# Attention by pairs of head pairs, and eight places for rounded products in a feed-forward pass

## The chip, the cores and the metric

The kernel runs on one core of one Trainium2 chip. The metric is the time of one execution in microseconds of device time (us). Lower is better. The core has five engines that run side by side and wait for each other through semaphores: PE (TensorE, matrix products and transposes through PSUM), DVE (VectorE), ACT (ScalarE), POOL (GpSimd) and SP (which here issues DMAs).

## The reference

Sixteen sequences of 128 tokens and width 256 go through one gated cross-attention layer and one gated, quantised feed-forward layer.

```
q, k, v   = heads of layernorm(x) Wq, ctx Wkv          # 16 heads of 64
k, v      = with one null key and value put in front    # 129 keys
out       = softmax(q k^T / 8) v, then Wout
x         = x + tanh(g_xattn) * layernorm(out) * ln_scale + ln_bias (gated too)
h         = act_qdq(layernorm(x))                       # one scale over the whole tensor
up, gate  = act_qdq(h w_up^T), act_qdq(h w_gate^T)      # 4 bit weights, 16 bit activations
gate      = act_qdq(gate * fixed_qdq_u16(sigmoid(gate)))
o         = act_qdq(gate * up)                          # the scale needs the maximum over all of o
x         = x + tanh(g_ffn) * (o w_down^T)
```

## The kernel before

**Attention.** The sixteen sequences are eight groups of two (`g` from 0 to 7; groups 1 to 5 are one loop body, groups 0, 6 and 7 are written out). The sixteen heads are eight head pairs (`c` from 0 to 7, `NS = 8`): two heads of 64 fill the 128 partitions. For a head pair the work goes from engine to engine:

- PE `scores(g, c)`: eight products of 64 rows into two PSUM banks of the pair's parity (`c % 2`).
- DVE `maxima(g, c)`: two reductions. ACT `exps(g, c)`: four exponentials with their row sums into `probs[c % 2]`. DVE `inverse_sums(g, c)`. POOL `normalise(g, c)`.
- PE `prob_transposes(g, c)`: four transposes into the one bank `pt_bank`. DVE `prob_copy(g, c)`: copies that bank into `pT[c % 2]`, and with this frees it.
- PE `values(g, c)`: eight products onto 64 columns of the array, into `pv_bank`. ACT `out_high` and DVE `out_low` split the result into two addends of reduced precision in `oT` (this split makes up for the precision of a float32r product; every projection is three products).

**What fills PE between.** Between these short pieces PE works off units of projections for the next group, in a hand-written order, `PLAN`. `Q0` to `Q7` make queries and keys (18 products of 256 columns), `V00` to `V11` values (12 products of 512 columns), `X` transposes of the normalised input, `F0` to `F8` transposes of the feed-forward weights in the last group, `W` the output projection (50 products). In the loop body steps 0 to 4 hold one `Q` each, step 5 holds `Q5` and `V00`, step 6 `Q6` and `V10`, step 7 `Q7` and `X`, and `V01`, `V11` and `W` are the tail. Group 6 holds `Q0` to `Q4`, `V00`, `Q5`, `Q6`, and `V10` and `W` as its tail. `unit` writes the banks `unit_bank`.

**DVE's work beside it.** Per step DVE also does one piece of the layernorms: in step 1 `attention_rstd`, in step 2 `attention_norm`, in step 3 `x2_statistics`, in step 4 `ln_stats`, in step 5 `ln_rstd`, in step 6 `ln_apply`. Groups 0 and 6 round one feed-forward weight each in three steps instead (`weight_scales`, `weight_integers`, `weight_values`; lines 1156 to 1160, 1165 and 1170). After `W` comes `attention_stats`. In this text a piece of this kind is DVE's side work of step `c`.

Each engine runs its instructions strictly in the order of the program; only semaphores tie them together.

**Feed-forward.** After the attention, the feed-forward layer makes `gate` and `up` (all 2048 tokens in SBUF, 24 pieces of 128x512 each) and goes over them in three passes, since each quantisation needs a maximum over everything. The third pass is the last part of the kernel. For piece `n` of 24 it needs the rounded product as int16, `oint(n)`: for even pieces DVE makes it (`o_integers`, line 1497) from two other int16 tiles that ACT (line 971, and line 968 for every third) and DVE (line 1478) remake; for odd ones ACT makes it from `up` (`prepare`, line 963). Then ACT casts it to the high addend (line 785), DVE makes the low addend (line 995) and counts `ol_ready`, and PE multiplies both by `w_down`: 12 products of 256 columns a piece (`down`, line 760). For the last six pieces PE does three piece by piece and then waits for all that are left. `oint(n)` has four places, in `tui`: place `n` is written again once the low addend of piece `n - 4` is done, which the code says as a wait for `n - 3` on `ol_ready`.

Of the kernel before, what the change touches and what calls it, by code (L numbers as in the profile page):

```python
# [72 lines left out]
def gated_cross_attention_ffn(nc, x, ctx, g_xattn, g_ffn, Wq, Wkv, null_kv, Wout, ln_scale, ln_bias,  # L73
                              w_gate, w_up, w_down, out):
    B, S, D = x.shape
# [32 lines left out]
    LOOPED = NG - 2  # L108

# [61 lines left out]
    with keep:  # L171
# [71 lines left out]
        GS = 6  # L243

# [232 lines left out]
        def oint(n):  # L477
            return tui[:, 2 + n % 4 // 2, n % 2 * HC:(n % 2 + 1) * HC]
# [75 lines left out]
        def _(pe):  # L554
# [8 lines left out]
            def unit(g, pos):  # L563
# [74 lines left out]
                else:  # L638
                    pe.wait_ge(w_free, g + 1)
                    for b in range(GB):  # L640
# [3 lines left out]
                        if b == 0:  # L644
                            wait(pe, ot_lo, g * NS + NS)
# [27 lines left out]
            def values(g, c):  # L673
                wait(pe, pt_copied, g * NS + c + 1)
                wait(pe, ot_lo, g * NS + c)
                for b in range(GB):
                    for h in range(2):
                        rows = slice(h * DH, (h + 1) * DH)
                        last = mm(pv_bank[rows, b * S:(b + 1) * S], v[:, b, c, rows],  # L679
                                  pT[:, c % 2, 2 * h + b, :], start=True, stop=True)  # L680
                last.then_inc(pv_done, 1)

            for pos in range(len(PRO)):
                unit("pro", pos)
                if PRO[pos] == "k6":
                    pe.wait_ge(null_ready, 1)
                    scores(0, 0)

            def group(g):
                final = isinstance(g, int) and g == NG - 1  # L690
                pos, (steps, tail) = 0, plan(g)
                for c in range(NS):
                    if c + 1 < NS:
                        scores(g, c + 1)
                    for _ in steps[c]:
                        unit(g, pos)
                        pos += 1
                    prob_transposes(g, c)
                    if c:
                        values(g, c - 1)  # L700
                if not final:
                    scores(g + 1, 0)
                values(g, NS - 1)
# [77 lines left out]
        def _(act):  # L781
# [27 lines left out]
            def out_high(g, c):  # L809
                wait(act, pv_done, g * NS + c + 1)  # L810
                high(oT[0][:, c, :], pv_bank[:, 0:TG]).then_inc(ot_hi, 1)
# [18 lines left out]
            while npos[0] < len(PRO):  # L830
                split("pro", npos[0])
                if PRO[npos[0]] == "k6":
                    exps(0, 0)
                if PRO[npos[0]] == "V11":
# [3 lines left out]
            def group(g):  # L838
                final = isinstance(g, int) and g == NG - 1
                pos, (steps, tail) = 0, plan(g)  # L840
                for c in range(NS):

                    weights = steps[c][0][0:1] == "F"
                    if c + 1 < NS and not weights:
                        exps(g, c + 1)
                    for _ in steps[c]:
                        split(g, pos)
                        pos += 1
                    if c + 1 < NS and weights:
                        exps(g, c + 1)  # L850
                    if c:
                        out_high(g, c - 1)
                if not final:
                    exps(g + 1, 0)
                out_high(g, NS - 1)
# [133 lines left out]
        def _(dve):  # L989
# [81 lines left out]
            def attention_stats(g, dst):  # L1071
# [9 lines left out]
                maxima(g + 1, 1)  # L1081
# [65 lines left out]
            def out_low(g, c):  # L1147
                dve.wait_ge(ot_hi, g * NS + c + 1)
                low(oT[1][:, c, :], pv_bank[:, 0:TG], oT[0][:, c, :]).then_inc(ot_lo, 1)
# [52 lines left out]
            while npos[0] < len(PRO):  # L1202
                if PRO[npos[0]] == "V00":
                    ln_stats(1)
                elif PRO[npos[0]] == "V10":
                    ln_rstd()
                elif PRO[npos[0]] == "V01":
# [6 lines left out]
                if PRO[npos[0]] == "k6":  # L1214
                    maxima(0, 0)
                    inverse_sums(0, 0)
# [4 lines left out]
            maxima(0, 1)  # L1221
            dve.wait_ge(const_ready, 1)

            def group(g):
# [3 lines left out]
                for c in range(NS):  # L1228
                    if 1 <= c < NS - 1:
                        maxima(g, c + 1)  # L1230
# [19 lines left out]
                    weights = steps[c][0][0:1] == "F"  # L1250
# [390 lines left out]
```

## Time and profile before

| | |
|---|---|
| time, median of 3 runs | 598.54 us (598.26 to 599.53) |
| the profiled execution's own time | 599.63 us |
| its span, first to last instruction | 597.6 us |
| PE busy | 524.0 us, 88% |
| DVE busy | 410.5 us, 69% |
| ACT busy | 298.4 us, 50% |
| POOL busy | 123.6 us, 21% |

The profiled execution took 2.0 us more than its span, and 1.1 us more than the median of the runs. The groups of the attention end at 99.7, 149.8, 199.9, 250.0, 300.1, 350.2, 392.2 and 431.4 us of the span, so one group of the loop body takes 50.1 us. The third feed-forward pass runs from 551 us to the end. Busy times of a PE whose products overlap are modelled, and so only a first hint. An engine's idle time costs something only where another engine waits for what comes late.

### The profile page before, as it was taken

How to read it: one execution, taken by the hardware profiler on the slowest of the kernel's cores; microseconds unless marked ns; L12 is line 12 of the kernel's file. 1: busy time of each engine (PE TensorE's matmuls, PEld its weight loads, DVE VectorE, ACT ScalarE, POOL GpSimd, SP SyncE). 2: the span in 40 equal slices, each digit the busy share in tenths (PEclk: the TensorE clock that was granted, in tenths of full speed). 3: DMA queues.
4: the chain of work that ended last, by engine and by line, in shares of the span. 5: the costliest groups of instructions: out<-in, count | busy, mean ns of one | idle time of the engine just before them, and what ended most of it. 6: DMA issues, size and time to landing. Idle time of an engine off the chain costs nothing. (4 is left out here: it accounts for less than half of the span.)

```text
span 597.6 us, 10965 instructions
## 1 busy us (share of the span) xinstructions
PE 524.0 (88%) x3921; PEld 456.4 (76%) x3921; DVE 410.5 (69%) x1077; ACT 298.4 (50%) x858; POOL 123.6 (21%) x137
## 2 busy tenths in 40 slices
PE   2999999999999999999999999997639999500997
PEld 2988889888988988888898898885528888400996
DVE  4779744754764574575476458658748989999685
ACT  3635532632542362363254335327325569897773
POOL 3001301220221130122022112213031029900000
PEclk9999999999999999999999999999959999855799
DMA  7922001101100110110110001005001000100033
GB/s 257 361 88 72 1 1 54 37 1 54 35 0 0 53 35 0 53 35 0 35 45 8 1 2 36 2 1 160 0 19 35 2 0 1 35 1 1 1 106 105
DMA packets 18478, 25.86 MB, mean 43 GB/s; under 512 B 1216, under 2 KB 15808, under 8 KB 18448
## 3 DMA queue, kind: packets, MB, share of 16 engines
q1 hardware_dynamic: 18192, 25.17, 12.8%
q0 software_dynamic: 256, 0.30, 0.2%
q8 instruction: 18, 0.29, 0.2%
q14 instruction: 12, 0.10, 0.1%
HBM read 21.27 MB, written 4.19 MB: 43 GB/s over the span
## 5 line engine op out<-in xcount | busy, mean ns | idle before, releaser
L804 ACT ACTIVATE probs<-bank,nmax 128x129 f32<-128x129 f32 x256 | 90.9, 368 | 117.8 <-DVE nmax L1132 117.7
L1551 POOL TENSOR_TENSOR probs<-probs,rinv 128x512 f32<-128x512 f32 x64 | 66.7, 1042 | 337.8 <-DVE rinv L1140 337.8
L607 PE MATMUL bank<-wv,ctxT 128*128 128x512 f32 x384 | 94.2, 397 | 0.0
L599 PE MATMUL bank<-ctxT,wk 128*128 128x256 f32 x672 | 88.9, 282 | 0.0
L599 PEld LDWEIGHTS bank<-ctxT,wk 128*128 128x128 f32 x672 | 83.6, 188 | 0.0
L607 PEld LDWEIGHTS bank<-wv,ctxT 128*128 128x128 f32 x384 | 70.5, 188 | 16.9 <-issue 1.2
L1144 DVE COPY pT<-bank 128x512 f32<-128x512 f32 x64 | 43.7, 682 | 20.7 <-PE bank L670 18.7
L599 PE MATMUL bank<-xnT,wq 128*128 128x256 f32 x336 | 54.7, 298 | 0.0
L785 ACT ACTIVATE oT<-bank 128x256 fp32r<-128x256 f32 x64 | 24.7, 386 | 60.0 <-PE bank L679 60.0
L804 ACT ACTIVATION_READ_ACCUMULATOR probs<-bank,nmax 128x1 f32 x256 | 52.0, 203 | 0.0
L599 PEld LDWEIGHTS bank<-xnT,wq 128*128 128x128 f32 x336 | 43.2, 188 | 7.2 <-issue 1.2
L1132 DVE TENSOR_REDUCE nmax<-bank 128x2 f32<-128x258 f32 x128 | 48.0, 416 | 0.0
L785 ACT ACTIVATE qk<-bank 128x512 f32<-128x512 f32 x64 | 38.4, 599 | 18.7 <-PE bank L599 13.6
L648 PE MATMUL bank<-wout,oT 128*128 128x256 f32 x384 | 47.1, 279 | 0.0
L1059 DVE TENSOR_TENSOR v<-bank,nvb 128x512 f32<-128x512 f32 x32 | 22.1, 690 | 35.7 <-PE bank L607 35.6
L648 PEld LDWEIGHTS bank<-wout,oT 128*128 128x128 f32 x384 | 46.0, 188 | 0.3
L662 PE MATMUL bank<-qk 64*128 64x130 f32 x512 | 45.9, 297 | 0.0
L679 PE MATMUL bank<-pT,v 128*64 128x128 f32 x512 | 42.1, 285 | 3.7 <-DVE oT L995 3.7
L760 PE MATMUL bank<-wd,oI 128*128 128x256 f32 x288 | 39.2, 298 | 5.4 <-DVE oI L995 5.2
L760 PEld LDWEIGHTS bank<-wd,oI 128*128 128x128 f32 x288 | 37.5, 204 | 7.2 <-DVE oI L995 6.5
L670 PE MATMUL bank<-ident,probs 128*128 128x128 f32 x256 | 38.6, 273 | 4.2 <-POOL probs L1551 4.2
L662 PEld LDWEIGHTS bank<-qk 64*128 64x128 f32 x512 | 33.6, 186 | 10.6 <-issue 9.2
(170 smaller groups left out, 810.6 us busy)
## 6 DMA issues: line engine op xcount, KB each, us to landing
craw<-in_ctx SPq DMA_DIRECT2D x8, 512.0 KB, 3.3
stage<-in_L_xattn_Wkv SPq DMA_DIRECT2D x8, 512.0 KB, 11.9
xa<-in_x SPq DMA_DIRECT2D x8, 256.0 KB, 2.7
xr<-in_x SPq DMA_DIRECT2D x8, 256.0 KB, 2.8
x_scratch<-y SPq DMA_DIRECT2D x7, 256.0 KB, 2.1
x2all<-x_scratch SPq DMA_DIRECT2D x1, 1792.0 KB, 8.3
xres<-x_scratch SPq DMA_DIRECT2D x6, 256.0 KB, 2.8
out<-yout SPq DMA_DIRECT2D x6, 256.0 KB, 2.2
```

The lines of the kernel that those rows point to most:

```text
L599: last = mm(bk[:, n * TG:(n + 1) * TG], wt[a][:, k, f], act_t[b][:, k, :], start=(k == 0 and i == 0), stop=(k == kk - 1 and i == len(TERMS ...
L607: last = mm(bk[:, :], ctxT[a][:, k, b * S:(b + 1) * S], wv[w][:, k, h * 512:(h + 1) * 512], start=(k == 0 and i == 0), stop=(k == KC - 1 a ...
L648: last = mm(o, oT[a][:, k, b * S:(b + 1) * S], wout[w][:, k, :], start=False, stop=(k == KF - 1 and i == len(TERMS) - 1))
L662: last = mm(score_bank[c % 2][h][:, b * QW:b * QW + QW], qk[rows, c, b, 0:S], qk[rows, c, GB + b, 0:QW], start=True, stop=True)
L670: last = nc.tensor.transpose(pt_bank[:, u * P:(u + 1) * P], probs[:, c % 2, u, 0:S], ident[:, :])
L679: last = mm(pv_bank[rows, b * S:(b + 1) * S], v[:, b, c, rows], pT[:, c % 2, 2 * h + b, :], start=True, stop=True)
L760: last = mm(bank[tg % 2 * 4 + t][:, 0:D], oI[a][:, tg % 2, j, t * P:(t + 1) * P], wd[w][:, j, :], start=(j == 0 and i == 0), stop=(j == KI ...
L785: return nc.scalar.activation(dst, src, act_copy, scale=scale)
L804: last = nc.scalar.activation(probs[:, c % 2, u, 0:NK], score_bank[c % 2][h][:, b * QW:b * QW + NK], ACT.Exp, bias=nmax[:, c % 2, u:u + 1] ...
L1132: last = V.tensor_reduce(nmax[:, c % 2, 2 * h:2 * h + 2], score_bank[c % 2][h][:, 0:GB * QW].rearrange("p (b s) -> p b s", b=GB)[:, :, 0:N ...
L1144: V.tensor_copy(pT[:, c % 2, :, :], pt_bank[:, :].rearrange("p (u s) -> p u s", u=4)).then_inc(pt_copied, 1)
L1551: G.tensor_tensor(probs[:, c % 2, :, 0:S], probs[:, c % 2, :, 0:S], rinv[:, c % 2, :].rearrange("p (u o) -> p u o", o=1).to_broadcast([P, ...
```

## The change

**In attention** the loop over eight head pairs becomes one over four pairs of them, `p` from 0 to 3 (`PAIRS = 4`). PE issues the scores of two head pairs in a row, and the two `values` in a row; `pv_bank` now takes both results (512 columns), and `out_high`, `out_low` are one instruction for both. Between stand the transposes of head pair `2p`, its units, the transposes of `2p + 1` and its units. The softmax of a head pair starts one pair ahead. On DVE the two `maxima` stand at the start of the pair, the side work (`beside(c)`) is put ahead of `prob_copy(g, c)`, and `inverse_sums` comes behind it. The last group issues its scores singly.

**In the third pass** `oint(n)` gets eight places, in `tpi` (which the second pass has done with), and the two waits for `n - 3` become waits for `n - 7`.

```diff
+    PAIRS = NS // 2
+        OR = 8
...
         def oint(n):
-            return tui[:, 2 + n % 4 // 2, n % 2 * HC:(n % 2 + 1) * HC]
+            return tpi[:, n % OR // 2, n % 2 * HC:(n % 2 + 1) * HC]
...
-            def values(g, c):
-                wait(pe, pt_copied, g * NS + c + 1)
-                wait(pe, ot_lo, g * NS + c)
...
+            def values(g, p):
+                wait(pe, pt_copied, g * NS + 2 * p + 2)
+                wait(pe, ot_lo, g * PAIRS + p)
...
@@ PE, group(g)
-                for c in range(NS):
-                    if c + 1 < NS:
-                        scores(g, c + 1)
-                    for _ in steps[c]:
-                        unit(g, pos)
-                        pos += 1
-                    prob_transposes(g, c)
-                    if c:
-                        values(g, c - 1)
-                if not final:
-                    scores(g + 1, 0)
-                values(g, NS - 1)
+                for p in range(PAIRS):
+                    to = (g, 2 * p + 2) if p + 1 < PAIRS else (None if final else (g + 1, 0))
+                    if to:
+                        scores(to[0], to[1])
+                        if not final:
+                            scores(to[0], to[1] + 1)
+                    for n in range(2):
+                        if n and to and final:
+                            scores(to[0], to[1] + 1)
+                        prob_transposes(g, 2 * p + n)
+                        for _ in steps[2 * p + n]:
+                            unit(g, pos)
+                            pos += 1
+                    values(g, p)
...
@@ DVE, group(g)
+                for p in range(PAIRS):
+                    to = (g, 2 * p + 2) if p + 1 < PAIRS else (None if final else (g + 1, 0))
+                    if to and not final:
+                        maxima(to[0], to[1])
+                        maxima(to[0], to[1] + 1)
+                    for n in range(2):
+                        c = 2 * p + n
+                        if to and final:
+                            maxima(to[0], to[1] + n)
+                        beside(c)
                         prob_copy(g, c)
-                        out_low(g, c - 1)
...
+                        if to:
+                            inverse_sums(to[0], to[1] + n)
+                        for _ in steps[c]:
+                            split(g, pos)
+                            pos += 1
+                    out_low(g, p)
...
@@ third pass, ACT and DVE
-                    wait(act, ol_ready, n - 3)
+                    wait(act, ol_ready, n - OR + 1)
...
-                wait(dve, ol_ready, n - 3)
+                wait(dve, ol_ready, n - OR + 1)
```

How PE's order moves in the loop body, at steps 3 and 4. L662 is `scores`, L599 the unit `Q`, L670 the transposes, L679 `values`. Before:

```order
L670 MATMUL bank<-ident,probs 128x128 [waits pt_copied,norm_done]
L679 MATMUL bank<-pT,v 64x128 [waits ot_lo,pt_copied]
L662 MATMUL bank<-qk 128x130 [waits exp_done]
L599 MATMUL bank<-xnT,wq 128x256 [waits unit_hi]
L599 MATMUL bank<-ctxT,wk 128x256 x12
...
L670 MATMUL bank<-ident,probs 128x128 [waits pt_copied,norm_done]
```

The same stretch now (L664, L601, L672 and L683 are the same four), over one whole pair:

```order
L664 MATMUL bank<-qk 128x130 [waits exp_done]
...
L664 MATMUL bank<-qk 128x130 [waits exp_done]
...
L672 MATMUL bank<-ident,probs 128x128 [waits pt_copied,norm_done]
...
L601 MATMUL bank<-xnT,wq 128x256 [waits unit_hi]
...
L672 MATMUL bank<-ident,probs 128x128 [waits pt_copied,norm_done]
...
L601 MATMUL bank<-xnT,wq 128x256 [waits unit_hi]
...
L683 MATMUL bank<-pT,v 64x128 [waits ot_lo,pt_copied]
```

Between one set of transposes and the next there stood the values, the scores and a unit; between the first and the second set of a pair there now stands a unit alone.

How DVE's order moves in the loop body at step 2 (oT is `out_low`, nmax `maxima`, rs and y the side work `attention_norm`, rinv `inverse_sums`, pT `prob_copy`). Before:

```order
L995 TENSOR_TENSOR oT<-bank,oT 128x256
L1132 TENSOR_REDUCE nmax<-bank 128x2 x2
L1006 SCALAR_TENSOR_TENSOR rs<-rs 128x2
...
L1105 SCALAR_TENSOR_TENSOR y<-y,rs,xr 128x256 x2
L1140 RECIPROCAL rinv<-rowsum 128x4
L1144 COPY pT<-bank 128x512
L995 TENSOR_TENSOR oT<-bank,oT 128x256
```

And now, from `out_low` of pair 0 to the copy of head pair 2:

```order
L998 TENSOR_TENSOR oT<-bank,oT 128x512
...
L1134 TENSOR_REDUCE nmax<-bank 128x2 x2
...
L1134 TENSOR_REDUCE nmax<-bank 128x2 x2
L1009 SCALAR_TENSOR_TENSOR rs<-rs 128x2
...
L1107 SCALAR_TENSOR_TENSOR y<-y,rs,xr 128x256 x2
L1146 COPY pT<-bank 128x512
L1142 RECIPROCAL rinv<-rowsum 128x4
```

Ahead of the copy there now stand the wide `out_low` of the pair before, twice the maxima and the side work.

## Rows read from the trace of the kernel before

**Rows 1.** The page: busy tenths of PE in 40 slices of the span.

```profile
PE   2999999999999999999999999997639999500997
```

**Rows 2.** Waits of PE over the span: us in total, times, longest.

```profile
PE bank L670 <- POOL probs L1551: 4.2, 4, 1.4
PE bank L679 <- DVE oT L995: 3.7, 8, 1.0
```

**Rows 3.** Timeline of PE in a body step: start, length, what.

```profile
206.10 0.60 PE L670 MATMUL bank<-ident,probs 128*128 128x128 f32 x4
206.63 0.66 PE L679 MATMUL bank<-pT,v 128*64 128x128 f32 x8
207.22 0.72 PE L662 MATMUL bank<-qk 64*128 64x130 f32 x8
...
208.69 1.58 PE L599 MATMUL bank<-ctxT,wk 128*128 128x256 f32 x12
210.11 0.60 PE L670 MATMUL bank<-ident,probs 128*128 128x128 f32 x4
```

**Rows 4.** Timeline of PE cut inside the scores that end at 207.94.

```profile
207.55 0.39 PE L662 MATMUL bank<-qk 64*128 64x130 f32 x4
...
207.66 0.28 PE L662 MATMUL bank<-qk 64*128 64x130 f32 x2
```

**Rows 5.** Timeline of DVE and PE at a wait of PE for DVE.

```profile
187.01 0.42 DVE L995 TENSOR_TENSOR oT<-bank,oT 128x256 fp32r<-128x256 f32 x1 [0.32 <-ACT oT L785]
187.35 0.68 DVE L995 TENSOR_TENSOR xnT<-bank,xnT 128x512 fp32r<-128x512 f32 x1
...
187.59 0.66 PE L679 MATMUL bank<-pT,v 128*64 128x128 f32 x8 [0.39 <-DVE oT L995]
```

**Rows 6.** Timeline of DVE in a body group.

```profile
199.89 0.76 DVE L1079 BATCH_NORM_STATS2 bn<-bank 128x6 f32<-128x256 f32 x2 [3.52 <-PE bank L648]
...
201.62 0.88 DVE L1089 SCALAR_TENSOR_TENSOR y<-bank,mv,gs 128x256 f32<-128x256 f32 x2
...
208.10 0.75 DVE L1132 TENSOR_REDUCE nmax<-bank 128x2 f32<-128x258 f32 x2
208.76 0.15 DVE L1006 SCALAR_TENSOR_TENSOR rs<-rs 128x2 f32<-128x2 f32 x1
...
210.92 0.17 DVE L1140 RECIPROCAL rinv<-rowsum 128x4 f32<-128x4 f32 x1
...
216.77 0.74 DVE L1028 BATCH_NORM_STATS2 bn<-xa 128x6 f32<-128x256 f32 x2
...
217.64 0.15 DVE L1032 BATCH_NORM_AGGREGATE mv<-bn 128x2 f32<-128x6 f32 x1
```

**Rows 7.** Timeline of DVE: weights in groups 0 and 6.

```profile
51.26 1.76 DVE L1170 TENSOR_TENSOR fraw<-fint,fs 128x1536 f32<-128x1536 int16 x1
...
367.06 1.74 DVE L1156 TENSOR_REDUCE fs<-fraw 128x48 f32<-128x1536 f32 x1
...
369.55 0.18 DVE L1140 RECIPROCAL rinv<-rowsum 128x4 f32<-128x4 f32 x1
```

**Rows 8.** The page's groups: copies out of PSUM.

```profile
L1144 DVE COPY pT<-bank 128x512 f32<-128x512 f32 x64 | 43.7, 682 | 20.7 <-PE bank L670 18.7
...
L785 ACT ACTIVATE qk<-bank 128x512 f32<-128x512 f32 x64 | 38.4, 599 | 18.7 <-PE bank L599 13.6
```

**Rows 9.** Timeline of PE in the third pass.

```profile
553.87 23.48 PE L760 MATMUL bank<-wd,oI 128*128 128x256 f32 x168 [3.64 <-DVE oI L995]
...
562.25 11.71 PE L760 MATMUL bank<-wd,oI 128*128 128x256 f32 x96
...
590.28 4.57 PE L760 MATMUL bank<-wd,oI 128*128 128x256 f32 x36 [0.89 <-DVE oI L995]
```

**Rows 10.** Busy by stretch: length, PE, PEld, DVE, ACT, POOL; PEclk, DMA share, GB/s.

```profile
560.00:573.96 13.96, 13.96 (x117) 13.75 (x115) 11.45 (x20) 10.92 (x19) 0.00 (x0) 1.00 0.15 47
573.96:590.28 16.32, 14.56 (x108) 13.30 (x108) 13.00 (x24) 11.48 (x20) 0.00 (x0) 1.00 0.32 96
```

More of the change, by code:

```diff
@@ L644, in unit @@
                         if b == 0:
[L645 removed]
+                            wait(pe, ot_lo, g * PAIRS + PAIRS)
                         for k in range(KF):
@@ L671, in prob_transposes @@
                 last.then_inc(pt_done, 1)
-            def values(g, c):
-                wait(pe, pt_copied, g * NS + c + 1)
-                wait(pe, ot_lo, g * NS + c)
[L676 to L680, printed above, removed]
+            def values(g, p):
[3 more added lines that the diff above has]
+                    c = 2 * p + n
+                    for b in range(GB):
+                        for h in range(2):
+                            rows = slice(h * DH, (h + 1) * DH)
+                            last = mm(pv_bank[rows, n * TG + b * S:n * TG + (b + 1) * S], v[:, b, c, rows],
+                                      pT[:, n, 2 * h + b, :], start=True, stop=True)
                 last.then_inc(pv_done, 1)
@@ L687, in _ @@
                     scores(0, 0)
+                    scores(0, 1)
             def group(g):
@@ L840, in group @@
                 pos, (steps, tail) = 0, plan(g)
[L841 to L855, printed above, removed]
+                for p in range(PAIRS):
+                    to = (g, 2 * p + 2) if p + 1 < PAIRS else (None if final else (g + 1, 0))
+                    for n in range(2):
+                        if to:
+                            exps(to[0], to[1] + n)
+                        for _ in steps[2 * p + n]:
+                            split(g, pos)
+                            pos += 1
+                    out_high(g, p)
                 for u in tail:
@@ L1215, in _ @@
                     maxima(0, 0)
-                    inverse_sums(0, 0)
+                    maxima(0, 1)
                 if PRO[npos[0]] == "V11":
@@ L1227, in group, with beside @@
                 pos, (steps, tail) = 0, plan(g)
-                for c in range(NS):
-                    if 1 <= c < NS - 1:
-                        maxima(g, c + 1)
+                def beside(c):
                     if c == 1 and not first:
@@ L1555, in _ @@
             normalise(0, 0)
+            normalise(0, 1)
             pool.wait_ge(const_ready, 1)
             def group(g):
-                for c in range(1, NS):
+                for c in range(2, NS):
                     if c == 6:
```

44 lines of the change are left out of this document (19 added, 25 removed).

## The prediction

> **What bounds the kernel now.** I read the slices first [rows 1]. PE's row is nines from the third slice to the 28th, so up to about 420 us PE decides, and after that it does in parts only. The waits say the same [rows 2]: over the whole span PE waited 3.7 us for `out_low` ahead of `values` (eight times, one a group) and 4.2 us for POOL ahead of transposes, the latter in four places of the last group. A group of the loop body takes 50.1 us and PE stands still for some 0.4 us of it. So in attention the change can only gain by making PE's own work shorter, and it loses whatever new wait it puts on PE. DVE has time to spare over a group, but what counts is when a single copy comes. In the third pass the timeline shows PE fed until 573.96 and then with holes, until it gets the last 36 products at 590.28 [rows 9].
>
> **What PE saves.** Ends of blocks are the measure, since one block's start overlaps the last one's end. From one end to the next [rows 3]: values 207.29 - 206.70 = 0.59 us, scores 207.94 - 207.29 = 0.65, unit Q 210.27 - 207.94 = 2.33, transposes 210.71 - 210.27 = 0.44; 4.01 for a step. Inside the scores, four products on two row halves take 0.39 and two take 0.28, so two cost 0.11 and all eight would take 0.44 [rows 4]. The same 0.11 for two products of 128 columns makes values 0.44. So the first products after a change of the array's shape cost extra: 0.15 for values (128x64), 0.21 for scores (64x128); the unit has no inside row here, and I take 0.20, so 2.13 without it. That is 0.56 a step for three changes, 0.19 each.
>
> Counting blocks in the two orders, a body group enters a new shape 25 times before (scores 8, values 8, full array 9) and 13 times after. Groups 0 to 6 save 12 each, the last saves 5 (23 to 18). 12 x 0.19 = 2.3 us a group. With the wait of 0.4 for `out_low` at the end of a group, which goes since the two results now leave together [rows 2], that is 2.7 us for each of seven groups.
>
> The Trainium skill says this too: TensorEngine Tiling (Array Packing), section Tiling Modes, states that changing the tiling mode drains the engine. The trace agrees, with the 0.15 to 0.21 above. Taken alone the rule says that half the changes is a faster kernel, and that is the rival below.
>
> **What PE loses.** Between the first and the second transposes of a pair there is now only one unit Q. The second ones write `pt_bank`, so they wait for DVE's copy of the first. DVE comes to this copy late: it must first do `out_low` of the pair before, which cannot start before `values` is over, then four reductions, then the side work of the even step.
>
> From the end of `values` to the end of the second transposes, on DVE's path: to ACT 0.04, `out_high` with 512 columns 0.60 (as the copy of a unit [rows 8]), to DVE 0.04, `out_low` 0.60 until the next can start (a low part of 512 columns is 0.68 long [rows 5]; a following instruction starts 0.08 before its end), two `maxima` 2 x 0.66 = 1.33 (208.10 to 208.76 [rows 6]), the side work B, the copy 0.68 [rows 8], then DVE to PE 0.15 and the block 0.66 (`oT` ends at 187.43, `values` starts at 187.59 [rows 5]). The sum is 4.10 + B. The handover to PE includes the weight load, which starts some 0.04 earlier, so I take 4.07 + B.
>
> On PE's own path: scores 0.65 + 0.44, transposes 0.44 + 0.15 for the change, unit 2.13, transposes 0.44: 4.25. So the wait is B - 0.18 when only one unit Q is in between.
>
> B in a body group [rows 6]: step 2, `attention_norm`, 208.76 to 210.92, 2.16, a wait of 2.0. Step 4, `ln_stats`, 216.77 to 217.79, 1.0, a wait of 0.8. Step 6 has V10 behind Q6, 2.8 us more of cover, no wait. Step 0 has no side work, but DVE comes from `attention_stats` of the group before: from the end of `W` 0.04, then 199.89 to 202.50 less the `maxima` inside and the overlap, 1.9, then 1.33, 0.68, 0.11 and 0.66, 4.7 against 4.25: 0.4. Together 3.2 us a group, against 2.7 saved. A body group becomes 0.5 us longer: five of them, +2.5.
>
> Side work of odd steps stands ahead of the second copy, which `values` waits for behind one more unit. `ln_rstd`, the longest, has Q5 and V00 in front of it; no wait. The softmax of a head pair now starts a pair (7 to 8 us) ahead; its exponentials wait for the transposes that free `probs`, its sum of ACT, DVE and POOL pieces is under 4 us, so it is not late in the body.
>
> Group 6: steps 4 to 6 round a weight. Step 4 is 2.5 us (367.06 to 369.55 [rows 7]), a wait of 2.3; step 6 is 1.7 (a 1.75 long instruction), with one Q in between here, 1.5; step 2 2.0; step 0 0.4. 6.2 - 2.7 = +3.5. Group 0: step 0 has 1.7 of weight work (51.26 [rows 7]), and DVE enters the group some 0.9 late, 1.1; step 1 has the 2.5 one, which makes the first `values` wait 0.5; step 2 1.5; step 4 0.8. 3.9 - 2.7 = +1.2.
>
> The last group is paced by the softmax chain. It has five changes less (1.0) and its first scores were issued before it (0.65), but the chain of a pair makes both the copy and `values` wait. Its waits now are 5 us [rows 2], and I estimate 0.7 more. -1.0, with bounds of -3 (no more waits) and +2.
>
> Attention: 1.2 + 2.5 + 3.5 - 1.0 = **+6.2 us**. The prologue gets the scores of head pair 1, 0.45 us, inside a stretch in which PE waits for DVE's weight work; nothing.
>
> **The third pass.** At full speed a product takes (11.71 - 0.28) / 95 = 0.12 us, a piece 1.44 [rows 9]. From 573.96 to the last end, 594.85, there are 12 pieces: 20.9 us against 17.3, so 3.6 us of holes. The rest of the pass PE was fed. Do DVE and ACT keep up, if the ring no longer stops them? From 560 to 590.28 they made the low parts of pieces 4 to 23: DVE was busy 24.45 us, 1.22 a piece, ACT 22.4, 1.12 [rows 10]. Both are below 1.44. Eight places give four more pieces of lead, so PE becomes the bound and its holes close: **-3.6 us**. Bounds: 0 if something else paces them, and -4.5 if the first pieces, which take PE longer (168 products in 23.48), run faster too. What comes after PE's last product is unchanged.
>
> **Sum:** 6.2 - 3.6 = +2.6 us. The profiled execution was 599.63, so one like it would take 602.2; against the median of the runs, 598.54 + 2.6 = **601.1 us**. A measurement of this kernel can tell about 0.2%, 1.2 us, from no change.
>
> **Rivals.**
> - *Faster: the changes of shape decide.* If DVE's copy came before PE needs it, attention would gain 2.7 x 7 + 1 to 2, some 20 us, and with the pass the kernel would take 575. For it: the saving is in PE's own rows. Against it: it needs B to be below 0.2 at steps 2 and 4, and B is 2.2 and 1.0 in the trace. In between, the sign turns where the waits are 2.6 us less over the program, that is 0.4 a group: an `out_high` or a handover that is a little quicker than I took, or a change that costs 0.22 instead of 0.19. Then 595 to 597.3. 0.12.
> - *No change to be told.* The same two sums, but each off by 1 to 2 us: 597.4 to 599.7. 0.20.
> - *Slower by more: the pass gives nothing.* If DVE's order (`finish` waits for PE's tiles) paces the third pass, or if the waits also reach `values` in the body, 604 to 606. Against it: DVE's busy share. 0.08.
> - *Slower as summed,* 599.8 to 604: 0.60.
>
> So slower has 0.68. The range of 597.4 to 604 leaves out the faster end and the part of the worst above 604. The unknown costs inside it: the change into `values` after a unit and into transposes after scores (0 to 0.21 each, some 30 of each, taken as 0.15), and the width of `out_high`.
>
> **What would show it.** In the profile after: a body group of 50.6 us in place of 50.1; PE waiting for DVE's copy (`pT`) ahead of transposes, three times a group, longest near 2.0, some 20 us in all plus 6 in group 6, with DVE's `values` wait gone from the body; two scores blocks back to back in 1.1 us from end to end, two `values` in 1.0; group 6 near 45.5 us. In the third pass PE's row without holes behind 574 and ACT's wait for DVE's `oI` gone; PE's last product 3.6 us earlier relative to its first. I am wrong if PE's waits for the copy stay under 2 us a group, or if the holes of the third pass stay.

## The result and the profile after

| | before | after |
|---|---|---|
| median of the runs | 599.03 us (598.26 to 599.65, 4 runs) | 605.75 us (602.39 to 609.66, 4 runs) |
| the profiled execution: time, span, mean granted clock | 599.63, 597.6, 0.951 | 605.15, 603.1, 0.951 |

The ratio is 1.0102, with an interval of 1.0068 to 1.0137. So the kernel became slower, as forecast, but by 6.7 us at the median and not by 2.6, and the median lies above the range that was given (597.4 to 604.0).

The page of the profile after. Its first line is the span, then the busy time of each engine, then two of the rows in 40 slices:

```profile
span 603.1 us, 10904 instructions
PE 509.5 (84%) x3921; PEld 453.5 (75%) x3921; DVE 412.7 (68%) x1045; ACT 295.5 (49%) x826; POOL 126.5 (21%) x137
...
PE   2998899899899989989998998798738999800698
PEclk9999999999999999999999999899877999965699
```

The row of nines of [rows 1] now has eights all through attention. PE waits there in every group. The 26th digit of the clock's row (377 to 392 us) and the 29th (422 to 437) are eights, in the last two groups of attention; this comes back below.

The waits of PE over the span (us in total, times, longest), kernel after:

```profile
PE bank L672 <- DVE pT L1146: 23.7, 25, 2.1
...
PE bank L683 <- DVE pT L1146: 6.2, 8, 2.3
PE bank L767 <- DVE oI L998: 3.6, 1, 3.6
```

The two rows of [rows 2] are gone: no wait for `out_low` and none for POOL. In their place PE waits for DVE's copy `pT`, 23.7 us ahead of transposes (L672), and 6.2 us ahead of values (L683). Of the third pass only the wait at its start is left.

PE in one body group (151.4 to 202.6), timeline: start, length, what, and the idle time ahead of it:

```profile
151.32 1.17 PE L664 MATMUL bank<-qk 64*128 64x130 f32 x16
152.42 0.66 PE L672 MATMUL bank<-ident,probs 128*128 128x128 f32 x4
...
155.58 0.63 PE L672 MATMUL bank<-ident,probs 128*128 128x128 f32 x4 [0.36 <-DVE pT L1146]
...
158.68 1.09 PE L683 MATMUL bank<-pT,v 128*64 128x128 f32 x16 [0.34 <-DVE pT L1146]
159.70 1.17 PE L664 MATMUL bank<-qk 64*128 64x130 f32 x16
...
165.34 0.63 PE L672 MATMUL bank<-ident,probs 128*128 128x128 f32 x4 [1.75 <-DVE pT L1146]
...
173.68 0.63 PE L672 MATMUL bank<-ident,probs 128*128 128x128 f32 x4 [0.70 <-DVE pT L1146]
```

Two scores now stand together (x16, and the next block begins 1.10 us behind their start), and two values too (158.68 to 159.70 by the starts, 1.02). The waits stand at steps 0, 2 and 4, where they were expected, and at one more place: the values of pair 0, at 158.68. This group takes 51.2 us, the five of the loop 51.1 on average.

PE in the third pass, timeline, kernel after:

```profile
563.45 36.93 PE L767 MATMUL bank<-wd,oI 128*128 128x256 f32 x288 [3.64 <-DVE oI L998]
```

All 288 products are one row without a hole. From the first start to the last end it is 36.93 us; in [rows 9] it was 594.85 - 553.87 = 40.98.

**Where the 5.5 us between the two profiled executions are.** I put the ends of the eight groups (the last end of the output products, L650) of both traces side by side. After: 100.3, 151.4, 202.6, 253.7, 304.9, 356.0, 403.0, 441.8. Before: 99.7, 149.8, 199.9, 250.0, 300.1, 350.2, 392.2, 431.4.

| stretch | before | after | difference | predicted |
|---|---|---|---|---|
| prologue and group 0 | 99.7 | 100.3 | +0.7 | +1.2 |
| five body groups, each | 50.1 | 51.1 | +1.03, together +5.1 | +0.5, together +2.5 |
| group 6 | 42.0 | 47.0 | +5.0 | +3.5 |
| last group | 39.2 | 38.7 | -0.5 | -1.0 |
| from there to the first product of the third pass | 122.5 | 121.7 | -0.8 | 0 |
| third pass, first start to last end | 40.98 | 36.93 | -4.05 | -3.6 |
| sum | | | +5.5 | +2.6 |

(The signs are right wherever one was forecast. The rows are rounded, the sum is not.) Two rows are off by over a microsecond: the body groups by 2.6, group 6 by 1.5.

### The profile page after: what moved, and what is told of

Read it like the earlier page. It is cut to its first block and busy times, and to the rows that moved or that the text cites. A ratio compares the mean times of both kernels' runs of the same rounds, so it can differ in the third digit from the quotient of the medians.

```text
span 603.1 us, 10904 instructions
## 1 busy us (share of the span) xinstructions
PE 509.5 (84%) x3921; PEld 453.5 (75%) x3921; DVE 412.7 (68%) x1045; ACT 295.5 (49%) x826; POOL 126.5 (21%) x137
## 5 line engine op out<-in xcount | busy, mean ns | idle before, releaser
L1551 POOL TENSOR_TENSOR probs<-probs,rinv 128x512 f32<-128x512 f32 x64 | 69.6, 1088 | 344.0 <-DVE rinv L1142 343.9
L609 PE MATMUL bank<-wv,ctxT 128*128 128x512 f32 x384 | 95.6, 402 | 0.0
L601 PE MATMUL bank<-ctxT,wk 128*128 128x256 f32 x672 | 89.0, 282 | 0.0
L601 PEld LDWEIGHTS bank<-ctxT,wk 128*128 128x128 f32 x672 | 83.8, 188 | 0.0
L672 PE MATMUL bank<-ident,probs 128*128 128x128 f32 x256 | 41.7, 286 | 23.7 <-DVE pT L1146 23.7
L1062 DVE TENSOR_TENSOR v<-bank,nvb 128x512 f32<-128x512 f32 x32 | 22.0, 689 | 48.9 <-PE bank L609 48.9
L601 PE MATMUL bank<-xnT,wq 128*128 128x256 f32 x336 | 53.9, 296 | 0.0
L672 PEld LDWEIGHTS bank<-ident,probs 128*128 128x128 f32 x256 | 27.8, 143 | 33.2 <-issue 28.5
L998 DVE TENSOR_TENSOR oT<-bank,oT 128x512 fp32r<-128x512 f32 x32 | 22.1, 691 | 39.3 <-ACT oT L792 39.3
L650 PE MATMUL bank<-wout,oT 128*128 128x256 f32 x384 | 47.3, 279 | 0.0
L650 PEld LDWEIGHTS bank<-wout,oT 128*128 128x128 f32 x384 | 46.2, 188 | 0.3
L1134 DVE TENSOR_REDUCE nmax<-bank 128x2 f32<-128x258 f32 x128 | 45.6, 416 | 0.0
L601 PEld LDWEIGHTS bank<-xnT,wq 128*128 128x128 f32 x336 | 43.6, 189 | 0.0
L683 PE MATMUL bank<-pT,v 128*64 128x128 f32 x512 | 35.0, 279 | 6.3 <-DVE pT L1146 6.2
L767 PE MATMUL bank<-wd,oI 128*128 128x256 f32 x288 | 36.9, 294 | 3.6 <-DVE oI L998 3.6
L664 PE MATMUL bank<-qk 64*128 64x130 f32 x512 | 38.1, 285 | 0.0
```

The lines of the kernel that those rows point to most:

```text
L601: last = mm(bk[:, n * TG:(n + 1) * TG], wt[a][:, k, f], act_t[b][:, k, :], start=(k == 0 and i == 0), stop=(k == kk - 1 and i == len(TERMS ...
L609: last = mm(bk[:, :], ctxT[a][:, k, b * S:(b + 1) * S], wv[w][:, k, h * 512:(h + 1) * 512], start=(k == 0 and i == 0), stop=(k == KC - 1 a ...
L650: last = mm(o, oT[a][:, k, b * S:(b + 1) * S], wout[w][:, k, :], start=False, stop=(k == KF - 1 and i == len(TERMS) - 1))
L664: last = mm(score_bank[c % 2][h][:, b * QW:b * QW + QW], qk[rows, c, b, 0:S], qk[rows, c, GB + b, 0:QW], start=True, stop=True)
L672: last = nc.tensor.transpose(pt_bank[:, u * P:(u + 1) * P], probs[:, c % 2, u, 0:S], ident[:, :])
L683: last = mm(pv_bank[rows, n * TG + b * S:n * TG + (b + 1) * S], v[:, b, c, rows], pT[:, n, 2 * h + b, :], start=True, stop=True)
```

## The experiments

Each ratio is against runs of the kernel before on the same chip. The first four below shared one chip and one set of such runs (599.32 us, 11 runs), the next four a second chip (598.28 us, 11 runs), and the last two a third (599.71 us, 9 runs).

### The same kernel again

No edit; more runs, to see the scatter and a second profile.

> The changed kernel once more, to see how its time scatters. Its first four runs took 602.4 to 609.7 us, where the kernel before took 598.3 to 599.7. Theory A (PE's new waits let the granted clock fall, at places that differ from run to run): again a scatter of 4 us or more, a longer time going with a lower mean clock, and in the profile short stretches at half clock between 355 and 442 us. Theory B (the waits alone make the time): the scatter stays under 2 us and the time does not follow the clock.

Measured: 605.14 us (602.55 to 606.41, 6 runs), ratio 1.0089 [1.0067, 1.0110]. In the second profile the body groups were 51.07 to 51.17 and group 6 was 47.06. I had tied the time of a run to its mean granted clock. That holds only loosely: 606.41 us came at 0.946 and 602.55 at 0.951, but 604.00 at 0.954. The groups repeat to 0.1 us, and the median is 5.8 to 6.7 us above before. The runs of this kernel scatter over 4 to 7 us, those of before over 1.4 to 3.2.

### Attention alone

The product ring goes back to four places, the rest of the change stays:

```diff
-        OR = 8
+        OR = 4
...
-            return tpi[:, n % OR // 2, n % 2 * HC:(n % 2 + 1) * HC]
+            return tui[:, 2 + n % 4 // 2, n % 2 * HC:(n % 2 + 1) * HC]
```

> The attention part alone; the rounded products of the third pass have four places again. If the two parts add up, it is slower than the changed kernel by what the third pass gained, 3.6 to 4.1 us: some 9 to 10 us above the kernel before, 608 to 610 us, with PE's holes behind the fifteenth piece of the third pass back. Rival: the gain of the third pass came from a clock that rose sooner because attention ended at another time; then it is within 1 us of the changed kernel.

Measured: 609.14 us (607.57 to 610.75, 5 runs), ratio 1.0173 [1.0152, 1.0195]. Attention alone costs 9.8 us at the median, not 6.2. Its third pass took 41.0 us from first start to last end and has the holes of [rows 9]. Its profiled execution (607.57 us) was the fastest of the five; there the prologue with group 0 is 1.2 us longer than before, the five body groups together 5.0, group 6 3.5, and the last group 0.9 shorter. The prediction had +1.2, +2.5, +3.5 and -1.0: in this profile the body groups alone are off.

### The third pass alone

Attention as before, the products of the third pass in eight places:

```diff
-            return tui[:, 2 + n % 4 // 2, n % 2 * HC:(n % 2 + 1) * HC]
+            return tpi[:, n % 8 // 2, n % 2 * HC:(n % 2 + 1) * HC]
```

with the waits for a free place moved from four products back to eight.

> The third pass alone: eight places, attention as in the kernel before. By the sum of the prediction 598.5 - 3.6 = 594.9 us, up to 594.4; PE's row in the third pass without holes. Rival (the eight places help only where the attention is by pairs): 598 to 599.

Measured: 595.59 us (593.21 to 596.30, 6 runs), ratio 0.9928 [0.9910, 0.9947], that is -3.7 us. The timeline of its third pass:

```profile
554.12 37.40 PE L760 MATMUL bank<-wd,oI 128*128 128x256 f32 x288 [3.64 <-DVE oI L995]
```

40.98 - 37.40 = 3.58 us. That term stood as summed, and so did its reason: before, ACT waited ten times for DVE's low part ahead of making a rounded product (L963), 7.6 us in all, and with eight places that wait is gone (in the profile after too). And the halves add up: +9.8 - 3.7 = +6.1, against +5.8 for the whole on the same chip. So the whole surprise is in attention.

### The copy ahead of the side work

The theory that DVE's side work (B) makes PE wait says that the copy, put first, brings back nearly all of it. A rival would be that two head pairs at a time cost PE something else, such as a softmax that comes too late; then the order on DVE would matter little.

```diff
-                        beside(c)
                         prob_copy(g, c)
+                        beside(c)
```

> The changed kernel with DVE's copy of the transposed probabilities ahead of its side work, in every step. Theory 1 (DVE's side work ahead of the copy is what makes PE wait, and the changes of the array's shape are a real saving): the waits of 1.7 and 0.7 us in a body group go, some 0.4 us at the group's start and at most 0.4 us ahead of the first values remain; a body group takes 51.1 - 3.9 + 0.5 to 0.9 = 47.7 to 48.1 us, group 6 40.5 to 41.5, and the kernel 575 to 580 us. Rival 2 (the wide copies out of PSUM and the four maxima alone make the copy late): groups stay above 50 us and the kernel above 598. Rival 3 (the shape changes save nothing, PE's row is only cut differently): about 595, that is the third pass alone.

Measured: 578.96 us (577.04 to 581.73, 6 runs), ratio 0.9659 [0.9633, 0.9685]: 26 us less than after, from one line. A body group takes 47.8 to 48.0, and group 6 takes 40.1, just below the expected 40.5 to 41.5. All waits of PE between 143 and 334 us, in this kernel:

```profile
PE bank L672 <- DVE pT L1146: 1.4, 4, 0.4
```

One wait of 0.4 is left per group, at step 0. The rival falls.

### The copy first in even steps only

```diff
+                        if n == 0:
+                            prob_copy(g, c)
                         beside(c)
-                        prob_copy(g, c)
+                        if n == 1:
+                            prob_copy(g, c)
```

This keeps the order of the odd steps, whose side work I had called free.

> The copy ahead of DVE's side work in even steps only; in odd steps the side work stays ahead. Theory 1 (the wait is the whole of the side work minus some 0.2 us, wherever it stands ahead of a copy that PE needs): the waits ahead of the second transposes go as with the copy first everywhere, but the side work of step 3 (1.3 us, behind that of step 2) now holds up the second copy and so the values of pair 1, by some 1.4 us; a body group 49.1 to 49.5 us, against 47.9 with the copy first everywhere and 51.1 in the changed kernel; the kernel 587 to 591. Rival (only the first copy matters, the second has a unit as cover): a body group as with the copy first everywhere, 48 us, the kernel 579.

Measured, on another chip (before 598.28): 592.72 us (591.22 to 594.71, 4 runs), ratio 0.9908 [0.9884, 0.9931]. The body group is 49.5 as expected; the kernel missed the expected 587 to 591 by 1.7 us, because group 6 only came down to 42.0 and the last group stayed at 39.0 (its clock fell there, beside a wait of 2.28). The waits of PE in a body group of this kernel (148.9 to 198):

```profile
PE bank L683 <- DVE pT L1146: 1.5, 2, 1.1
PE bank L672 <- DVE pT L1146: 0.4, 1, 0.4
```

Both waits of L683 are those of the values, which odd copies make. So the odd steps' side work wasn't free: with the even copies early, it costs 49.5 - 47.9 = 1.6 us a group, partly since PE now arrives at the values sooner.

### The first reciprocals of a pair later

Why do the values of pair 0 wait? DVE's timeline of the kernel after, at steps 0 and 1:

```profile
155.82 0.18 DVE L1142 RECIPROCAL rinv<-rowsum 128x4 f32<-128x4 f32 x1 [0.39 <-ACT probs L811]
155.91 0.14 DVE L1004 TENSOR_SCALAR rs<-mv 128x2 f32<-128x2 f32 x1
156.09 1.06 DVE L1005 TENSOR_SCALAR rs<-rs 128x2 int32<-128x2 int32 x1
157.18 0.16 DVE L1009 SCALAR_TENSOR_TENSOR rs<-rs 128x2 f32<-128x2 f32 x1
...
157.85 0.69 DVE L1146 COPY pT<-bank 128x512 f32<-128x512 f32 x1
```

and POOL's timeline there:

```profile
156.08 1.04 POOL L1551 TENSOR_TENSOR probs<-probs,rinv 128x512 f32<-128x512 f32 x1 [16.97 <-DVE rinv L1142]
```

The instruction of L1005 works on 128x2 elements and took 1.06 us. It begins 0.01 us behind POOL's multiply and ends 0.02 us behind POOL's end (157.12). The multiply waits for `inverse_sums` (L1142). That of the even step now stands right ahead of the side work of the odd step, so the two meet each time. If POOL holds this instruction back, then with these reciprocals behind the side work it should be short, and the wait of the values should go:

```diff
+                        if n == 1 and to:
+                            inverse_sums(to[0], to[1])
                         prob_copy(g, c)
-                        if to:
-                            inverse_sums(to[0], to[1] + n)
+                        if n == 1 and to:
+                            inverse_sums(to[0], to[1] + 1)
```

> The changed kernel with one instruction moved: the inverse sums of the first head pair of a pair stand behind the side work of the odd step instead of ahead of it, so POOL's multiplication starts when that side work is over. In the changed kernel the second small instruction of steps 1 and 5 took 1.06 us in every body group, and 0.17 in the kernel before; it began just before POOL's multiplication and ended just before it did. Theory A (POOL's multiplication holds up this DVE instruction): it is back to 0.17 us, the wait of 0.34 us ahead of the values of pair 0 goes, a body group 50.6 to 50.8 us in place of 51.1, the kernel 602 to 603.5. Rival B (the small instruction is slow for another reason, such as the place behind a wide copy): it stays at 1.06 us and the group at 51.1.

(By the rows above the instruction begins just behind the start of the multiply and ends just behind its end, not before them.)

DVE's timeline at the same place of this kernel:

```profile
155.22 0.16 DVE L1004 TENSOR_SCALAR rs<-mv 128x2 f32<-128x2 f32 x1
155.41 0.17 DVE L1005 TENSOR_SCALAR rs<-rs 128x2 int32<-128x2 int32 x1
...
156.21 0.18 DVE L1142 RECIPROCAL rinv<-rowsum 128x4 f32<-128x4 f32 x1
156.30 0.69 DVE L1146 COPY pT<-bank 128x512 f32<-128x512 f32 x1
```

And all waits of PE in its four groups from 151 to 354 us:

```profile
PE bank L672 <- DVE pT L1146: 11.2, 12, 1.8
```

L1005 is back to 0.17 us, there is no wait of values any more, and a body group takes 50.7 instead of 51.1. In the time of the kernel it can't be told: 602.98 us (601.10 to 605.17, 6 runs), ratio 1.0078 [1.0056, 1.0100], whose interval overlaps that of after. Five groups at 0.4 would be 2 us; the ratios differ by 0.0011, which is 0.7 us.

### The waits filled in the last two groups

The second thing that I had left out is the clock. This kernel adds products that nothing reads ahead of the late transposes of group 6 and the late values of the last group, so that PE has work in its waits:

```diff
+            def fill(g, p, count):
+                wait(pe, ot_lo, g * PAIRS + p)
+                for _ in range(count):
+                    mm(pv_bank[:, 0:256], wq[0][:, 0, 0:P], wq[0][:, 0, 0:256], start=True, stop=True)
...
+                        if isinstance(g, int) and g == NG - 2 and n == 1 and p:
+                            fill(g, p, (0, 12, 15, 9)[p])
...
+                    if final and p in (1, 2):
+                        fill(g, p, 15)
```

> The changed kernel with PE kept busy in its longest waits of the last two groups: 12, 15 and 9 products that nothing reads ahead of the second transposes of pairs 1 to 3 of group 6, and 15 each ahead of the values of pairs 1 and 2 of group 7. Each fill is shorter than the wait it stands in by its row. Theory A (these waits let the granted clock fall): no stretch at half clock between 350 us and the end of attention, group 6 45.4 to 45.6 us in the profile, group 7 under 38.3, the median 602 to 603.5 with a scatter under 2.5 us. Rival B (the clock falls for another reason, or costs nothing): scatter and median as in the changed kernel, 605.

Busy time by stretch of group 6, kernel after (length, then PE, PEld, DVE, ACT, POOL with their instructions, granted clock, share of DMA, GB/s):

```profile
376.00:380.00 4.00, 1.87 (x16) 1.65 (x15) 3.90 (x7) 1.51 (x8) 0.73 (x1) 1.00 0.00 0
380.00:384.00 4.00, 4.00 (x12) 2.87 (x10) 1.62 (x3) 1.49 (x8) 2.78 (x2) 0.57 0.00 0
384.00:388.00 4.00, 4.00 (x48) 3.56 (x48) 2.77 (x7) 1.28 (x5) 0.00 (x0) 1.00 0.00 0
```

The same stretch in the filled kernel:

```profile
380.00:384.00 4.00, 4.00 (x28) 3.19 (x30) 2.90 (x4) 1.51 (x8) 3.51 (x2) 1.00 0.00 0
```

And PE's timeline there, kernel after:

```profile
379.26 0.63 PE L672 MATMUL bank<-ident,probs 128*128 128x128 f32 x4 [2.13 <-DVE pT L1146]
379.64 4.59 PE L609 MATMUL bank<-wv,ctxT 128*128 128x512 f32 x12
```

then in the filled kernel:

```profile
377.71 1.95 PE L678 MATMUL bank<-wq 128*128 128x256 f32 x15
379.99 0.63 PE L672 MATMUL bank<-ident,probs 128*128 128x128 f32 x4 [0.33 <-DVE pT L1155]
380.38 3.04 PE L609 MATMUL bank<-wv,ctxT 128*128 128x512 f32 x12
```

Behind the wait of 2.13 us the granted clock is 0.57 as the mean of four microseconds, so for most of them the lower of its two levels (1.2 GHz) held, and the same twelve products took 4.59 us instead of 3.04. With the wait filled the clock stays at 1.00, and group 6 takes 45.5 us instead of 47.0. Attention alone (above) had no such fall in group 6 of its profile, behind a wait of 2.12 us, and its group 6 also took 45.5. The second profile of the changed kernel and that of the kernel with the later reciprocals had it there (group 6 47.1 and 46.9, waits of 2.13 and 2.12). So nearly the same wait brings the fall in some executions and not in others.

Measured: 603.59 us (602.78 to 604.83, 6 runs), ratio 1.0084 [1.0070, 1.0098]. The runs scatter over 2.0 us in place of 3.9 (the same kernel again) or 7.3 (the first four), but the median, 0.1 above the expected 602 to 603.5, isn't separated from that of after by these intervals.

### Both, the copy first and filled

The copy ahead of side work, and `fill` with 7 and 16 products ahead of the values of pairs 1 and 2 of the last group, again read by nothing.

> The copy first in every step, and 7 and 16 such products ahead of the values of pairs 1 and 2 in the last group, where that kernel waits 1.1 and 2.3 us and where its clock fell. If the falls are the reason for its scatter of 577.0 to 581.7: 576.5 to 577.5 us with a scatter under 2 us. Rival: no difference, 579.

Measured: 577.63 us (576.18 to 578.68, 5 runs), ratio 0.9649 [0.9632, 0.9667]. The last group takes 37.2 instead of 38.1, and no stretch of attention is at the lower clock. The median is just above the expected 576.5 to 577.5, the scatter 2.5 instead of under 2. The ratio isn't separated from that of the copy first alone (0.9633 to 0.9685), so what filling gives is read from the last group and not from the time of the kernel.

### The second scores moved back

To measure what a change of the array's shape costs, apart from waits, I took the kernel with the copy first and let the second scores of a pair stand behind the first transposes, in groups 0 to 6. That is two more changes a pair, eight a group.

```diff
                         scores(to[0], to[1])
-                        if not final:
-                            scores(to[0], to[1] + 1)
...
                         prob_transposes(g, 2 * p + n)
+                        if n == 0 and to and not final:
+                            scores(to[0], to[1] + 1)
```

> The kernel with the copy first in every step (578.96 us, a body group 47.9), with the second scores of a pair moved behind the first transposes of the pair, in groups 0 to 6. The same products; the array's shape changes twice more a pair. DVE still gets the second scores about when it is through with the first maxima. If a change of shape costs 0.15 to 0.21 us: 4 x 0.4 = 1.6 us more a group at least in PE's own work, a body group 49.3 to 49.9, the kernel 590 to 593. Rival (the saving came from fewer waits and handovers, not from the shape): the group stays within 0.4 us of 47.9 and the kernel within 3 us of 579.

Measured (before 599.71 here): 587.04 us (585.70 to 588.58, 4 runs), ratio 0.9802 [0.9771, 0.9832]. PE's timeline in a body group:

```profile
147.31 0.72 PE L664 MATMUL bank<-qk 64*128 64x130 f32 x8
147.95 0.66 PE L672 MATMUL bank<-ident,probs 128*128 128x128 f32 x4
148.54 0.72 PE L664 MATMUL bank<-qk 64*128 64x130 f32 x8
149.19 0.98 PE L601 MATMUL bank<-xnT,wq 128*128 128x256 f32 x6
```

A body group takes 49.0 us and PE waits nowhere in it. I had expected 49.3 to 49.9, since I didn't see that the wait of 0.4 at step 0 would go too: the scores in between give DVE that time. The kernel came below the expected 590 to 593.

The last group is the same here as with the copy first alone, and this profile has no fall of the clock in it, behind the same wait:

```profile
407.56 1.10 PE L683 MATMUL bank<-pT,v 128*64 128x128 f32 x16 [2.26 <-DVE pT L1146]
```

It took 37.2 us, as with the wait filled, and 38.1 with the copy first alone, where the clock fell. So that fall cost 0.9 us, and filling gained only what it cost.

### The copy ahead of the maxima

The last wait is that of step 0, so there the copy goes ahead of the maxima as well; the rest is as in the kernel with copy first and filled.

```diff
+                    early = p == 0 and not final
+                    if early:
+                        prob_copy(g, 0)
                     if to and not final:
                         maxima(to[0], to[1])
                         maxima(to[0], to[1] + 1)
...
-                        prob_copy(g, c)
+                        if c or not early:
+                            prob_copy(g, c)
                         beside(c)
```

> The kernel with the copy first and the last group's waits filled (577.63 us), with DVE's copy at the start of a group also ahead of the four maxima. It waits there 0.36 us in each of seven groups, for a copy that stands behind the statistics of the output and the maxima, 1.3 us. If that is the whole wait, it goes: 577.6 - 7 x 0.4 = 574.8 us. Rival (the later maxima make the exponentials and the first values late by as much): 577 to 578.

Measured, on the same chip: 574.43 us (573.63 to 575.12, 5 runs), ratio 0.9584 [0.9561, 0.9607]. This is the fastest kernel of the study, 4.2% faster than before. Its body group takes 47.42 us without a wait of PE. Neither kernel has a wait of PE in the body, so eight changes of shape cost 49.04 - 47.42 = 1.62 us, 0.20 each.

## Why the prediction was right and wrong

**What PE saves: right.** The term was 12 x 0.19 = 2.3 us a group. The body group of before without its wait is 50.1 - 0.4 = 49.7, that of the last experiment 47.4: 2.3 us. The price of one change, read from ends of blocks in [rows 3] and [rows 4], was 0.19; eight of them taken back cost 0.20 each. (If the wait of before also cost the 0.14 found below, 2.15 us are left for twelve changes, 0.18 each.)

**Where PE waits for the copy, and how long: right for even steps.** The idle times in the rows above are 0.36, 0.34, 1.75 and 0.70, together 3.15 us. The group lost 51.13 - 47.42 = 3.71, so each of the four waits costs about 0.14 more than the row shows as idle. The likely reason is the overlap of two blocks, which is lost as well: transposes that waited end 0.63 us behind their own start, and without a wait they end 0.44 behind the end of the block ahead of them. With it: 0.5 at step 0 (predicted 0.4, though its terms, 4.7 against 4.25, make nearly 0.5), 1.9 at step 2 (2.0), 0.8 at step 4 (0.8). That it is DVE's order and no late softmax is shown by the kernel with the copy first.

**The step that failed in the body.** "`ln_rstd`, the longest, has Q5 and V00 in front of it; no wait." The sum thus put the waits of `values` in the body at nothing. I looked at the longest side work of an odd step and not at `attention_rstd` in step 1, which has only one unit ahead of the values. It would have been in time by its own length; but POOL's multiply held one of its instructions back by 0.9 us, and the values of pair 0 waited 0.34 us by the row (0.48 with the overlap) in every group. This and the 0.1 us at step 0 make a group 1.03 us longer instead of 0.5, five groups 2.6 us. The reciprocals moved later took 0.4 us of this away, and the group of 50.7 that they leave is 3.3 us above the last experiment's, where the prediction had 3.2 of waits. The rows that could have warned me are in the trace of before:

```profile
170.67 0.29 DVE L1001 TENSOR_SCALAR rs<-mv 128x2 f32<-128x2 f32 x1
```

and on POOL:

```profile
169.65 1.28 POOL L1562 TENSOR_TENSOR xr<-xr,gb 128x512 f32<-128x512 f32 x1
```

L1001, the first small instruction of the same side work, took 0.29 us in six such places, where it takes 0.16 otherwise, and ended 0.03 us behind POOL's end. I hadn't read POOL's timeline beside DVE's. I had even named "the waits also reach `values` in the body" as the rival of 0.08 and 604 to 606 us; the median of the first four runs did go there, but of the two reasons that rival gave, only the one on `values` came true, in part; the third pass gained what was summed.

**Group 6: the wait was right, the clock was left out.** 45.5 us were predicted, and 45.5 it took in both kernels with this order whose profile had no fall of the clock there; 46.9 to 47.1 in the three with one. The prediction had no word on the clock, though it put three waits of 1.5 to 2.3 us into group 6 alone. What the falls cost at the median remains open: in the profile filling the waits gains 1.5 us in group 6, in the time of the kernel the gain is not separable. The wide scatter of the changed kernel fits falls that come in some executions, and with filled waits it was narrower (2.0 us); over so few runs that is a sign and no proof.

**Group 0 and the last group.** Group 0 by itself took 51.4 us in place of 50.1: +1.3, against +1.2 predicted. The table has +0.7 because the prologue ended at 48.9 us in place of 49.6; over the traces of this study it ended at 48.6 to 50.1, so I take that for scatter. The last group was 0.5 off, and 0.1 off in the profile of attention alone. The last group of the profile after also had a fall at 428 us, behind a wait of 2.26; with the waits filled it took 38.1 instead of 38.7. With the copy first it took 38.1 with a fall and 37.2 without one, so a fall there costs 0.9.

**The third pass: right.** -3.6 predicted, -3.6 in the profile of the pass alone, -3.7 in its time. In the profile of the whole change it was -4.05; there the clock rose 4.8 us after the first product instead of 5.8, which saves half of that 1 us. The gate pass ahead of it was 0.8 us shorter, where the clock rose 3.9 us after its first product and not 5.7. I had no rows from which to forecast either.

**The rival "faster"** (575 us) had the right sum for its condition: it asked for a DVE copy that comes before PE needs it. The change doesn't do this, one moved line does, and gives 579; with the last wait and the falls away it is 574.4.

## What to carry to other kernels

Fewer changes of the array's shape are worth 0.2 us each here, but only if what PE then meets sooner is ready: when two steps are joined, follow the copies that free PSUM through the queue of the engine that makes them, and put them ahead of work that nobody waits for. Look at every side work with the least cover in front of it, not at the longest one. Read the small instructions of DVE beside POOL's timeline, and waits of around 2 us on PE beside the granted clock behind them.

## What the hardware showed that I had not expected

**A small DVE instruction can last as long as POOL's multiply.** L1005 took 1.05 to 1.06 us in all 12 places of the profile after where POOL's multiply (1.04 us) had begun 0.01 us earlier. Of the other three places it took 0.17 us in two and 0.34 in the prologue, where POOL issued DMAs and multiplied nothing. With the copy first, L1004 met the multiply midway; DVE's timeline of that kernel:

```profile
150.12 0.30 DVE L1004 TENSOR_SCALAR rs<-mv 128x2 f32<-128x2 f32 x1
150.45 0.17 DVE L1005 TENSOR_SCALAR rs<-rs 128x2 int32<-128x2 int32 x1
```

and POOL's:

```profile
149.34 1.04 POOL L1551 TENSOR_TENSOR probs<-probs,rinv 128x512 f32<-128x512 f32 x1 [16.97 <-DVE rinv L1142]
```

It ended at 150.42, POOL at 150.38. Wherever L1004 or L1005 met a multiply, their end is 0.02 to 0.04 us behind POOL's by these rows. Not every instruction is held: BATCH_NORM_AGGREGATE on 128x2 elements took its usual 0.18 us at 166.00 in the profile after, while POOL multiplied from 165.36 to 166.41. The copy out of PSUM (0.69 at 156.30, reciprocals later) ran beside the multiply at 156.46 at its usual length. The other way round it holds too. DVE in group 6 of the profile after, then POOL:

```profile
379.11 1.73 DVE L1168 TENSOR_TENSOR fint<-fraw,fs 128x1536 int16<-128x1536 f32 x1
```

```profile
379.27 2.47 POOL L1551 TENSOR_TENSOR probs<-probs,rinv 128x512 f32<-128x512 f32 x1 [4.95 <-DVE rinv L1142]
```

DVE was first here, and the multiply took 2.47 us instead of 1.04, its last 0.90 behind DVE's end. The Trainium skill has the rule: SBUF — State Buffer, section SBUF: two separate sides, says that DVE and GpSimd share a pair of SBUF ports as an exclusive lock for a whole instruction, which a DVE operation in a mode with two ports, or with two inputs from SBUF, needs; whichever comes first blocks the other. The trace agrees both ways, 1.06 against 0.17 us and 2.47 against 1.04; in which mode L1005 ran, no run here shows.

**The clock fell beside waits of 1.95 to 2.3 us.** The granted clock of group 6 is shown above. In the profile of the kernel with the copy first it fell in the last group, right behind this row:

```profile
399.60 1.86 PE L683 MATMUL bank<-pT,v 128*64 128x128 f32 x16 [2.26 <-DVE pT L1146]
```

This block takes 1.09 us at full clock. In the ten profiles of kernels with pairs, PE had 14 waits of 1.95 to 2.28 us in the last two groups. The clock went to the lower level at nine of them, from 0.2 us before the end of the wait to 1.3 behind it, and not at the other five. It fell at none of the waits of 1.7 to 1.8 us in the body groups (five in each of five profiles). The Trainium skill, TensorE: Matmul & The Clock Gate, section Why this matters for your kernels, advises against idle gaps between bursts of products above a bound that is longer than any wait of PE in these groups. Keeping below that bound was not enough: the falls came at gaps of 1.95 to 2.3 us, with shorter waits around them, and only in some executions. What decides which of them brings a fall stays open.
